# Shifted-window attention block on one core: moving a projection ahead of a weighed sum, norm sums ahead of an addition, and splitting an exp in two

## The chip, the cores and the metric

The kernel runs on one core of one Trainium2 chip. The metric is device time in microseconds (us), the median of several executions. Five engines take part, each with its own queue of instructions in program order: PE (TensorE: matmuls and transposes; its weight loads are shown apart as PEld), DVE (VectorE), ACT (ScalarE), POOL (GpSimd) and SP, which issues the DMAs. They are tied together by semaphores that the program sets by hand.

## The reference, cut to what matters

A block of a Swin-style transformer on x of shape (32, 32, 32, 64): 32 images of 32 x 32 tokens with 64 channels, windows of 8 x 8 tokens shifted by 4, 4 heads of 16.

```python
h = _ln(x, ln1_g, ln1_b); h = roll(h, (-4, -4)); win = windows(h, 8)     # 512 windows of 64 tokens
q, k, v = split(win @ qkv_w + qkv_b, 3)                                # per head 64 x 16
attn = softmax(q @ k.T * 16 ** -0.5 + rel_pos_bias + shift_mask)       # 64 x 64 per head
out = roll(unwindow((attn @ v) @ proj_w + proj_b), (4, 4))
x = x + out
h2 = _ln(x, ln2_g, ln2_b)
return x + gelu(h2 @ fc1_w + fc1_b) @ fc2_w + fc2_b
```

Everything is float32.

## The kernel before

The 32 images form 8 groups of 4. The attention half is one unrolled loop over `n`, 64 steps of half an image's windows ("pairs") and 4 more (`TAIL`) to drain; 8 steps make a group. Every engine has its own copy of the loop, and the order in which its code is written is the order of its queue. The feed-forward half (fc1, gelu, fc2) follows in a loop of its own.

On PE, one step holds some of these blocks:

- `score(image)`, at odd `n` alone: the 64 passes q·k for both pairs of the next image, into `scores[0]` and `scores[1]`. The keys come from `kX`, which SP's DMAs spread from `kT`.
- `weigh(n - 2)`: the weighed sum, probabilities times values, from `probsT` into `outs`. It waits for the exp of that pair (`probsT_ready`) and for the quotient before it (`outs_taken`).
- `fill(...)`: everything that uses the two PSUM banks `work`. `TASKS` lists them: "XT" (eight transposes of normed x), "QK" (queries and keys of one image), "V" (values), "Y" (output projection of half a group). A fill waits until the fill before it in the list was copied out of `work`: "QK" follows either an XT, which ACT copies (`xT_copied`), or a Y, which DVE adds to x (`y_added`); "V" follows a QK, which ACT copies (`kT`, then `qT`: `q_copied`).
- `transpose_probs(n - 1)`: eight 128 x 128 transposes of the shifted scores into `trans`, which are the same two banks as `scores[0]`. They wait for POOL's shift, for DVE's `scores_taken` on the image that was just scored, and for the exp of the pair before.
- `transpose_o(n - 3)`: two transposes of the quotient.

Per step, DVE runs `bias_and_max(n)` (L483 adds the bias to the scores, L489 takes row maxima), `divide(n - 3)` (L496, L498), at steps 7 and 1 of a group (counted from 0) `add_y` (L534, or three pieces at L540: adds the projection to x), `norm(n)` (sums for the layer norm: L412, L418), and at steps 3 and 5 `add_y_bias` (L524). POOL shifts the scores by the maxima (L373) and does the other steps of the norm. ACT runs the exp (L645: one instruction over `trans`, 1024 columns), copies the transposed quotient (L653) and empties `work` (L605 xT, L610 kT, L612 qT, L619 vX).

An XT stands at the end of steps 2 and 4 of a group, a Y at the end of steps 6 and 0, a QK in each odd step, a V after the transposes of each odd step. So in a steady group two of the four QKs follow an XT (steps 3 and 5) and two a Y (steps 7 and 1).

Of the kernel before, what the change touches and what calls it, by code (L numbers as in the profile page):

```python
# [8 lines left out]
ACT = mybir.ActivationFunctionType  # L9
# [3 lines left out]
P = 128  # L13
# [11 lines left out]
PAIRS = STEPS * GROUPS  # L25
BANK = 512
# [41 lines left out]
TR, PV, OUT = 1, 2, 3  # L68
# [33 lines left out]
def tasks_at(n):  # L102
    return [task[1:] for task in TASKS if task[0] == n]
# [12 lines left out]
def ln_at(stage, n):  # L116


    found = []
    for group in range(1, GROUPS + 1):  # L120
        steps = LN_STEPS_FIRST if group == 1 else LN_STEPS
        found += [(group, i) for i, at in enumerate(steps[stage])
                  if at is not None and STEPS * (group - 1) + at == n]
    return found
# [7 lines left out]
def build(nc, x_d, params_d, out_d):  # L132
    with ExitStack() as ctx:
        def sb(name, *shape, dtype=F32):
            return ctx.enter_context(nc.sbuf_tensor(name, [P, *shape], dtype))

        def sem(name):
            return ctx.enter_context(nc.semaphore(name))
# [6 lines left out]
        trans = scores[0]  # L145
# [12 lines left out]
        probs = [sb(f"probs{i}", 2 * BANK) for i in range(4)]  # L158
        probsT = [sb(f"probsT{i}", 2 * BANK) for i in range(2)]
# [13 lines left out]
        ident = sb("ident", P)  # L173
# [38 lines left out]
        trans_ready, probsT_ready = sem("trans_ready"), sem("probsT_ready")  # L212
# [39 lines left out]
        def means_before(G, i):  # L252

            if G == 0:
                return 1
            return 1 + 3 * (G - 1) + (1, 1, 2, 3)[i]
# [153 lines left out]
        def _(dve):  # L410
# [5 lines left out]
            def square_sum(u, r):  # L416
                dve.wait_ge(ln_squares, u + 1)
                nc.vector.tensor_reduce(stat_sq[:, r * WIN:(r + 1) * WIN],  # L418
                                        squares[r % PIECES][:, :].rearrange("q (a f) -> q a f", f=C),
                                        AXX, ALU.add).then_inc(ln_sq, 1)  # L420
# [7 lines left out]
            for t in range(2):  # L428
                done = nc.vector.memset(vX[t][:, :, :], 0.0)
# [4 lines left out]
            for column in ones:  # L434
                done = nc.vector.memset(column, 1.0)
# [6 lines left out]
            for half, i in ((second_half, 1), (first_half, 2), (second_half, 2), (first_half, 3),  # L442
                            (second_half, 3)):
                dst, src, c0, n = half(0, i)
                done = nc.vector.tensor_tensor(  # L445
                    dst, src.rearrange("q (a f) -> q a f", f=C),
                    stat_mean[:, c0:c0 + n].unsqueeze(2).to_broadcast([P, n, C]), ALU.add)
# [55 lines left out]
            def norm(n):  # L503
                for group, i in ln_at("square_sum", n):
                    square_sum(PIECES * group + i, i)
                for group, i in ln_at("sum", n):
                    if group == GROUPS:
                        sum2(i)
                        continue
                    if i == 0:  # L510
                        dve.wait_ge(x_loaded[group % 2], 16 * COPIES * (group // 2 + 1))
                        dve.wait_ge(ln_mean, means_before(group - 1, 3))
                    row_sum(x[:, group * ROW + i * PIECE:][:, 0:PIECE], i)

            def sum2(s):

                dve.wait_ge(ln_mean, MEANS + max(s - 3, 0))
                row_sum(x[:, s * PIECE:(s + 1) * PIECE], s % PIECES)
# [36 lines left out]
            for n in range(PAIRS + TAIL):  # L555
                if n < PAIRS:
                    bias_and_max(n)
                if 0 <= n - OUT < PAIRS:
                    divide(n - OUT)

                for kind, of, i in tasks_at(n - 0.5):
                    if kind == "Y":
                        add_y(of, i)
                norm(n)
                if n < PAIRS and n % STEPS in (3, 5):
                    add_y_bias(n // STEPS, (n % STEPS - 3) // 2)
            for kind, of, i in tasks_at(PAIRS + TAIL - 0.5):
# [24 lines left out]
        def _(act):  # L592
# [48 lines left out]
            squares_of(-1)  # L641

            def exp(n):
                act.wait_ge(trans_ready, n + 1)
                nc.scalar.activation(probsT[n % 2][:, :], trans, ACT.Exp)\  # L645
                  .then_inc(probsT_ready, 1)

            def copy_oT(n):
                act.wait_ge(oT_ready, n + 1)
# [45 lines left out]
        def _(pe):  # L695
            def mm(out, lhsT, rhs, start=True, stop=True):
                return nc.tensor.matmul(out, lhsT, rhs, start=start, stop=stop)  # L697
# [55 lines left out]
            for t in range(2):  # L753
                mm(scores2[:, 3 + t:4 + t], w1raw[0:C, t * P:(t + 1) * P], shift[0:C, 1:2], stop=False)
                done = mm(scores2[:, 3 + t:4 + t], ident[:, :], bf1_raw[:, t:t + 1], start=False)
# [9 lines left out]
            def score(image):  # L765

                two = image % 2
                if image:
                    pe.wait_ge(kX_loaded[two], 16 * KX_DMAS * ((image + 1) // 2))
                else:  # L770
                    pe.wait_ge(first_keys, 2)
                copied("QK", image // GI, image % GI)
                if image:
                    pe.wait_ge(scores_taken, 2 * image)
                if image > 1:
                    pe.wait_ge(probsT_ready, 2 * image - 2)
                for u in range(2):
                    for p in range(2):
                        for k in range(2):
                            at = (2 * k + u) * P + p * N  # L780
                            for w in range(2):
                                half = w ^ k
                                for hh in range(2):

                                    rows = slice(32 * (2 * w + hh), 32 * (2 * w + hh + 1))
                                    out = scores[k][half * N:(half + 1) * N, hh * BANK + u * 256:][:, 0:256]\
                                        .rearrange("q (h p m) -> q p h m", h=2, p=2)[:, p]
                                    done = mm(out, qT[two][rows, at:at + N], kX[two][rows, :, at:at + N])
                done.then_inc(scores_ready, 1)

            def transpose_probs(n, image):

                pe.wait_ge(shifted, n + 1)
                pe.wait_ge(scores_taken, 2 * image + 1)
                if n:
                    pe.wait_ge(probsT_ready, n)
                for t in range(8):
                    done = nc.tensor.transpose(trans[:, t * P:(t + 1) * P],  # L798
                                               probs[n % 4][:, t * P:(t + 1) * P], ident[:, :])
                done.then_inc(trans_ready, 1)  # L800

            def weigh(n):
                image, k = divmod(n, 2)
                if k == 0:
                    copied("V", image // GI, image % GI)
                pe.wait_ge(probsT_ready, n + 1)
                if n:
                    pe.wait_ge(outs_taken, n)
                else:
                    pe.wait_ge(y_bias_made, 1)  # L810
                for u in range(2):
                    for h in range(HEADS):
                        for w in range(2):
                            at = (u * HEADS + h) * P + (w ^ k) * N
                            row = (w * 4 + 2 * k + u) * HEADS + h
                            out = outs[w * N:(w + 1) * N, u * HEADS * VW:(u + 1) * HEADS * VW]\
                                .rearrange("q (p h d) -> q p h d", p=2, h=HEADS)[:, :, h]
                            done = mm(out, probsT[n % 2][:, at:at + N], vX[image % 2][:, row, :])
                done.then_inc(outs_ready, 1)
# [28 lines left out]
            for n in range(PAIRS + TAIL):  # L848
                if n % 2 and n + 1 < PAIRS:
                    score((n + 1) // 2)  # L850
                if 0 <= n - PV < PAIRS:
                    weigh(n - PV)
                if n % 2:
                    for kind, of, i in tasks_at(n):
                        fill(kind, of, i)
                if 0 <= n - TR < PAIRS:
                    transpose_probs(n - TR, min((n + 1) // 2, PAIRS // 2 - 1))
                if 0 <= n - OUT < PAIRS:
                    transpose_o(n - OUT)
                if n % 2 == 0:  # L860
                    for kind, of, i in tasks_at(n):
                        fill(kind, of, i)
                for kind, of, i in tasks_at(n + 0.5):
                    fill(kind, of, i)
                if n in (PAIRS, PAIRS + 1):
                    transpose_piece(n - PAIRS)

            pe.wait_ge(w1_ready, 1)
            pe.wait_ge(probsT_ready, PAIRS)
            pe.wait_ge(oT_copied, PAIRS)  # L870
            copied("Y", GROUPS - 1, 1)

# [74 lines left out]
```

## Time and profile before

| | us |
|---|---|
| median of 3 runs | 503.17 |
| the runs | 503.17, 503.45, 500.56 |
| the profiled execution | 500.17 |
| span in the profile | 498.4 |
| busy in the span: PE, DVE, POOL, ACT | 436.9, 383.7, 378.2, 294.9 |
| share of the chain that ended last: PE, DMA, ACT, DVE | 71%, 9%, 8%, 2% |

The profiled execution took 500.17 us, of which 1.8 us lie outside its span. The loop over pairs runs from about 34 us to 346 us of the span, the feed-forward half after it. "Idle before" in a row of a timeline is the time for which that engine had been idle, and the name behind the arrow is what ended it; "issue" stands there when the profile shows no releaser. The chain is the profile's walk back from the last instruction to what released each one.

### The profile page before, as it was taken

The numbers are of one execution on the slowest core, as the hardware profiler recorded it, in microseconds if no ns is written. First come the engines' busy times: TensorE is split into PE (matmuls) and PEld (weight loads), VectorE is DVE, ScalarE is ACT, GpSimd is POOL, SyncE is SP. The second block draws the span as 40 slices with busy tenths as digits, with TensorE's granted clock in tenths as the row PEclk, the third lists the DMA queues.
The fourth block names the chain that finished last, engine by engine and source line by source line (L and its number), as shares of the span: only waits on it lengthen the run. The fifth ranks groups of instructions, "written<-read, shape, count | busy, mean of one in ns | idle before, by whom it ended". The sixth has DMA issues, their size and how long they took to land.

```text
span 498.4 us, 21474 instructions
## 1 busy us (share of the span) xinstructions
PE 436.9 (88%) x9630; PEld 329.1 (66%) x9630; DVE 383.7 (77%) x549; ACT 294.9 (59%) x437; POOL 378.2 (76%) x376
## 2 busy tenths in 40 slices
PE   0665978899999899999999999787999999999995
PEld 0542756687777777777777767675566676667664
DVE  2767697889999999899999989965467766777652
ACT  1233665675765665666657646543777677767761
POOL 2658989988988989989889799730588888888830
PEclk9995999999999999999999999999999999999999
DMA  8300523511411511511111101100011321330333
GB/s 166 68 1 22 130 64 69 122 30 26 118 34 26 125 29 24 130 25 27 41 26 35 35 24 31 39 3 3 3 40 49 87 59 30 87 78 11 87 90 81
DMA packets 9986, 27.10 MB, mean 54 GB/s; under 512 B 3368, under 2 KB 3368, under 8 KB 7976
## 3 DMA queue, kind: packets, MB, share of 16 engines
q1 hardware_dynamic: 9896, 25.74, 22.0%
q8 instruction: 76, 1.25, 1.1%
q14 instruction: 14, 0.11, 0.1%
HBM read 9.21 MB, written 8.39 MB: 35 GB/s over the span
## 4 chain that ended last, share of the span: by engine, by line
PE 71%; DMA 9%; ACT 8%; SPq 4%; issue 4%; DVE 2%; ACTq 0%; DVEq 0%
PE work L697 26%; PE outs L697 17%; PE scores L697 16%; DMA kX<-kT 5%; PE scores L798 5%; ACT kT L610 4%; PE scores L838 4%; SPq L283 3%; DMA params<-in_params 2%; ACT qT L612 2%; PE work L712 2%; DMA x<-in_x 1%; PE outs L826 1%; ACT probsT L645 1%; SPq L275 1%
## 5 line engine op out<-in xcount | busy, mean ns | idle before, releaser
L373 POOL TENSOR_TENSOR probs<-probs,negmax 128x1024 f32<-128x1024 f32 x64 | 123.8, 1934 | 27.2 <-DVE negmax L489 27.1
L339 POOL TENSOR_TENSOR stat_rstd<-stat_var,minus_half 128x8 f32<-128x8 f32 (+1 forms) x62 | 104.9, 1691 | 5.0
L483 DVE TENSOR_TENSOR probs<-scores,bias 128x1024 f32<-128x1024 f32 x64 | 77.9, 1217 | 14.2 <-PE scores L697 14.2
L645 ACT ACTIVATE probsT<-scores 128x1024 f32<-128x1024 f32 x64 | 65.6, 1025 | 28.8 <-PE scores L798 28.8
L344 POOL TENSOR_TENSOR xn<-x,stat_mean 128x256 f32<-128x256 f32 (+1 forms) x91 | 78.1, 876 | 4.1
L697 PE MATMUL outs<-vX,probsT 128*64 128x34 f32 x2048 | 72.2, 225 | 9.4 <-issue 8.3
L489 DVE TENSOR_REDUCE negmax<-probs 128x16 f32<-128x1024 f32 x64 | 78.1, 1220 | 2.2
L697 PEld LDWEIGHTS outs<-vX,probsT 128*64 128x64 f32 x2048 | 65.9, 138 | 19.1 <-issue 19.0
L697 PEld LDWEIGHTS work<-params,probs 128*64 128x64 f32 x2048 | 62.3, 138 | 23.5 <-DVE x L577 20.5
L798 PEld LDWEIGHTS scores<-ident,probs 128*128 128x128 f32 x512 | 55.5, 142 | 28.1 <-issue 24.2
L610 ACT ACTIVATE kT<-work,bqkv 128x512 f32<-128x512 f32 x31 | 21.3, 688 | 86.6 <-PE work L697 86.6
L798 PE MATMUL scores<-ident,probs 128*128 128x128 f32 x512 | 70.6, 282 | 1.7 <-issue 1.7
L697 PE MATMUL work<-params,probs 128*64 128x64 f32 x2048 | 66.6, 223 | 0.0
L418 DVE TENSOR_REDUCE stat_sq<-squares 128x8 f32<-128x512 f32 x64 | 43.1, 681 | 28.2 <-ACT squares L597 28.0
L697 PE MATMUL scores<-kX,qT 32*64 32x128 f32 x2048 | 39.5, 282 | 15.6 <-DVE probs L483 5.6
L412 DVE TENSOR_REDUCE stat_sum<-x 128x8 f32<-128x512 f32 x64 | 42.2, 676 | 9.6 <-DMA x<-in_x 9.5
L597 ACT ACTIVATE squares<-xn 128x512 f32<-128x512 f32 x64 | 39.7, 630 | 15.7 <-DVE xn L445 15.3
L682 ACT ACTIVATE probs<-scores,bf 128x1024 f32<-128x1024 f32 x32 | 35.6, 1114 | 20.9 <-PE scores L697 20.8
L336 POOL TENSOR_TENSOR stat_var<-stat_sq,eps 128x8 f32<-128x8 f32 (+1 forms) x62 | 23.2, 375 | 31.6 <-DVE stat_sq L418 31.6
L697 PEld LDWEIGHTS scores<-kX,qT 32*64 32x64 f32 x2048 | 32.0, 133 | 22.5 <-DMA kX<-kT 14.5
L329 POOL TENSOR_TENSOR stat_mean<-stat_sum,one_over_c 128x8 f32<-128x8 f32 (+2 forms) x54 | 17.4, 322 | 33.6 <-DVE stat_sum L412 30.4
L619 ACT ACTIVATE vX<-work 64x512 f32<-64x512 f32 x64 | 39.0, 610 | 4.8 <-PE work L697 4.4
(61 smaller groups left out, 662.4 us busy)
## 6 DMA issues: line engine op xcount, KB each, us to landing
kX<-kT SPq DMA_DIRECT2D x124, 64.0 KB, 2.0
x<-in_x SPq DMA_DIRECT2D x32, 224.0 KB
out<-x SPq DMA_DIRECT2D x28, 224.0 KB
x<-in_x SPq DMA_DIRECT2D x32, 32.0 KB
out<-x SPq DMA_DIRECT2D x28, 32.0 KB
out<-x SPq DMA_DIRECT2D x16, 56.0 KB
params<-in_params SPq DMA_DIRECT2D x1, 805.5 KB, 12.0
out<-x SPq DMA_DIRECT2D x16, 8.0 KB
```

What stands on the lines that cost most here:

```text
L339: nc.gpsimd.tensor_tensor(stat_rstd[:, cols], stat_var[:, cols], minus_half[:, cols], ALU.pow).then_inc(ln_rstd, pieces)
L344: return nc.gpsimd.tensor_tensor(dst, src.rearrange("q (a f) -> q a f", f=C), m, ALU.add)
L373: nc.gpsimd.tensor_tensor(e, e, top, ALU.add).then_inc(shifted, 1)
L412: nc.vector.tensor_reduce(stat_sum[:, r * WIN:(r + 1) * WIN], src.rearrange("q (a f) -> q a f", f=C), AXX, ALU.add, negate=True).then_inc( ...
L418: nc.vector.tensor_reduce(stat_sq[:, r * WIN:(r + 1) * WIN], squares[r % PIECES][:, :].rearrange("q (a f) -> q a f", f=C), AXX, ALU.add).t ...
L483: nc.vector.tensor_tensor(e[:, :].rearrange("q (u a m) -> q a u m", u=2, a=2), scores[k].rearrange("q (a u m) -> q a u m", a=2, u=2), b.re ...
L489: nc.vector.tensor_reduce(negmax[n % 4][:, :], e[:, :].rearrange("q (a m) -> q a m", m=N), AXX, ALU.max, negate=True).then_inc(negmax_read ...
L597: nc.scalar.activation(squares[j % PIECES][:, :], xn[:, j * PIECE:(j + 1) * PIECE], ACT.Square, scale=float(C) ** -0.5).then_inc(ln_square ...
L610: nc.scalar.activation(kT[par][:, :], work[1], ACT.Identity, bias=bqkv[:, 1:2])\
L645: nc.scalar.activation(probsT[n % 2][:, :], trans, ACT.Exp)\
L697: return nc.tensor.matmul(out, lhsT, rhs, start=start, stop=stop)
L798: done = nc.tensor.transpose(trans[:, t * P:(t + 1) * P], probs[n % 4][:, t * P:(t + 1) * P], ident[:, :])
```

## The change

PE: in an odd step the fills of whole number `n` (the QK) now stand ahead of `weigh` and no longer behind it. ACT: the exp is two instructions of 512 columns, and each waits for its own four transposes. PE's transposes signal after every four, and each four wait for the half of the exp before that read their bank; `weigh` waits for one half ahead of each half of its matmuls. DVE: `norm(n)` now stands ahead of `add_y`. The work done is otherwise the same.

```diff
@@ DVE
+                norm(n)
                 for kind, of, i in tasks_at(n - 0.5):
                     if kind == "Y":
                         add_y(of, i)
-                norm(n)
@@ ACT
             def exp(n):
-                act.wait_ge(trans_ready, n + 1)
-                nc.scalar.activation(probsT[n % 2][:, :], trans, ACT.Exp)\
-                  .then_inc(probsT_ready, 1)
+                for half in range(2):
+                    cols = slice(half * BANK, (half + 1) * BANK)
+                    act.wait_ge(trans_ready, 2 * n + half + 1)
+                    nc.scalar.activation(probsT[n % 2][:, cols], trans[:, cols], ACT.Exp)\
+                      .then_inc(probsT_ready, 1)
@@ PE, score and transpose_probs
-                    pe.wait_ge(probsT_ready, 2 * image - 2)
+                    pe.wait_ge(probsT_ready, 2 * (2 * image - 2))
...
-                if n:
-                    pe.wait_ge(probsT_ready, n)
-                for t in range(8):
-                    done = nc.tensor.transpose(trans[:, t * P:(t + 1) * P],
-                                               probs[n % 4][:, t * P:(t + 1) * P], ident[:, :])
-                done.then_inc(trans_ready, 1)
+                for half in range(2):
+                    if n:
+                        pe.wait_ge(probsT_ready, 2 * n - 1 + half)
+                    for t in range(4 * half, 4 * (half + 1)):
+                        done = nc.tensor.transpose(trans[:, t * P:(t + 1) * P],
+                                                   probs[n % 4][:, t * P:(t + 1) * P], ident[:, :])
+                    done.then_inc(trans_ready, 1)
@@ PE, weigh
-                pe.wait_ge(probsT_ready, n + 1)
...
                 for u in range(2):
+                    pe.wait_ge(probsT_ready, 2 * n + u + 1)
@@ PE, the loop
-                if 0 <= n - PV < PAIRS:
-                    weigh(n - PV)
                 if n % 2:
                     for kind, of, i in tasks_at(n):
                         fill(kind, of, i)
+                if 0 <= n - PV < PAIRS:
+                    weigh(n - PV)
```

On PE, in step 7 of a group, behind a Y (`work<-params,oT`): the queue before, with what each block waits for. `work<-xT,wqkv` is the QK, `outs<-vX,probsT` the weighed sum, L798 the transposes.

```order
167 L697 MATMUL work<-params,oT 64x64 x31
168 L697 MATMUL scores<-kX,qT 64x2x64 [waits scores_taken,probsT_ready,q_copied,kX_loaded0]
169 L697 MATMUL scores<-kX,qT 64x2x64 x31
170 L697 MATMUL outs<-vX,probsT 64x2x17 [waits outs_taken,probsT_ready]
171 L697 MATMUL outs<-vX,probsT 64x2x17 x15
172 L697 MATMUL work<-xT,wqkv 64x512 [waits y_added]
173 L697 MATMUL work<-xT,wqkv 64x512 x3
174 L798 MATMUL scores<-ident,probs 128x128 [waits probsT_ready,scores_taken,shifted]
175 L798 MATMUL scores<-ident,probs 128x128 x7
```

And the same place now (line numbers are shifted by two or three):

```order
219 L699 MATMUL work<-params,oT 64x64 x31
220 L699 MATMUL scores<-kX,qT 64x2x64 [waits scores_taken,probsT_ready,q_copied,kX_loaded0]
221 L699 MATMUL scores<-kX,qT 64x2x64 x31
222 L699 MATMUL work<-xT,wqkv 64x512 [waits y_added]
223 L699 MATMUL work<-xT,wqkv 64x512 x3
224 L699 MATMUL outs<-vX,probsT 64x2x17 [waits probsT_ready,outs_taken]
225 L699 MATMUL outs<-vX,probsT 64x2x17 x7
226 L699 MATMUL outs<-vX,probsT 64x2x17 [waits probsT_ready]
227 L699 MATMUL outs<-vX,probsT 64x2x17 x7
228 L801 MATMUL scores<-ident,probs 128x128 [waits probsT_ready,scores_taken,shifted]
229 L801 MATMUL scores<-ident,probs 128x128 x3
230 L801 MATMUL scores<-ident,probs 128x128 [waits probsT_ready]
```

The QK with its wait for `y_added` has moved up by one block, so that only the scores stand between the Y and it, and the weighed sum is queued behind it.

On DVE, the same step before, from the quotient to the next scores:

```order
220 L498 TENSOR_TENSOR o_rows<-outs,inverse 128x256
221 L534 TENSOR_TENSOR x<-work,x 128x2x512
222 L418 TENSOR_REDUCE stat_sq<-squares 128x8
223 L483 TENSOR_TENSOR probs<-scores,bias 128x2x2x256
224 L489 TENSOR_REDUCE negmax<-probs 128x16
```

Now:

```order
220 L498 TENSOR_TENSOR o_rows<-outs,inverse 128x256
221 L418 TENSOR_REDUCE stat_sq<-squares 128x8
222 L534 TENSOR_TENSOR x<-work,x 128x2x512
223 L483 TENSOR_TENSOR probs<-scores,bias 128x2x2x256
224 L489 TENSOR_REDUCE negmax<-probs 128x16
```

The norm's sum and the addition to x have changed places.

## Rows read from the trace of the kernel before

**Rows 1.** Busy us of each engine in one stretch: start:end, length, then PE, PEld, DVE, ACT, POOL.

```profile
222.00:254.00 32.00, 30.24 (x763) 23.97 (x758) 29.82 (x40) 19.17 (x32) 28.07 (x26) 1.00 0.11 28
```

**Rows 2.** Timeline of PE, one image with an XT ahead: start, us, line, what.

```profile
204.00 1.21 PE L697 MATMUL scores<-kX,qT 32*64 32x128 f32 x64 [0.56 <-DMA kX<-kT]
205.13 1.13 PE L697 MATMUL outs<-vX,probsT 128*64 128x34 f32 x32
...
207.21 1.09 PE L798 MATMUL scores<-ident,probs 128*128 128x128 f32 x8
208.14 0.38 PE L826 MATMUL outs<-ident,o_rows 128*128 128x128 f32 x2
208.66 0.70 PE L697 MATMUL work<-wqkv,xT 64*64 64x64 f32 x32
209.63 1.13 PE L697 MATMUL outs<-vX,probsT 128*64 128x34 f32 x32 [0.27 <-issue]
...
211.61 0.38 PE L826 MATMUL outs<-ident,o_rows 128*128 128x128 f32 x2
211.83 1.04 PE L712 MATMUL work<-ident,xn 128*128 128x128 f32 x8
212.99 1.20 PE L697 MATMUL scores<-kX,qT 32*64 32x128 f32 x64
```

**Rows 3.** Timeline of ACT in the same stretch.

```profile
207.93 0.68 ACT L612 ACTIVATE qT<-work,bqkv 128x512 f32<-128x512 f32 x1
208.50 1.02 ACT L645 ACTIVATE probsT<-scores 128x1024 f32<-128x1024 f32 x1
209.41 0.39 ACT L653 ACTIVATE oT<-outs 128x256 f32<-128x256 f32 x1
...
211.81 1.03 ACT L645 ACTIVATE probsT<-scores 128x1024 f32<-128x1024 f32 x1 [0.91 <-PE scores L798]
...
213.00 1.03 ACT L605 ACTIVATE xT<-work 128x1024 f32<-128x1024 f32 x1
```

**Rows 4.** Waits of the whole span: total us, times, longest.

```profile
PE outs L697 <- issue: 8.3, 28, 0.9
...
PE scores L697 <- DMA kX<-kT: 3.8, 7, 1.3
PE scores L697 <- ACT probsT L645: 3.3, 4, 1.0
```

**Rows 5.** Timeline of DVE, steps 5 to 1 of that group.

```profile
213.05 1.93 DVE L524 TENSOR_TENSOR x<-x,y_bias 128x1024 f32<-128x1024 f32 x1
214.90 1.21 DVE L483 TENSOR_TENSOR probs<-scores,bias 128x1024 f32<-128x1024 f32 x1
...
222.13 1.23 DVE L534 TENSOR_TENSOR x<-work,x 128x1024 f32<-128x1024 f32 x1 [0.54 <-PE work L697]
223.27 0.68 DVE L418 TENSOR_REDUCE stat_sq<-squares 128x8 f32<-128x512 f32 x1
223.87 1.21 DVE L483 TENSOR_TENSOR probs<-scores,bias 128x1024 f32<-128x1024 f32 x1
...
231.15 1.36 DVE L540 TENSOR_TENSOR x<-work,x 128x512 f32<-128x512 f32 x3 [0.59 <-PE work L697]
```

**Rows 6.** Timeline of PE, later blocks of that group and the next group's scores.

```profile
216.22 1.06 PE L798 MATMUL scores<-ident,probs 128*128 128x128 f32 x8
...
222.00 1.21 PE L697 MATMUL scores<-kX,qT 32*64 32x128 f32 x64
...
240.60 1.21 PE L697 MATMUL scores<-kX,qT 32*64 32x128 f32 x64 [0.36 <-DMA kX<-kT]
```

**Rows 7.** Timeline of POOL around the row of 213.05 us above.

```profile
212.00 1.90 POOL L373 TENSOR_TENSOR probs<-probs,negmax 128x1024 f32<-128x1024 f32 x1 [0.28 <-DVE negmax L489]
213.86 1.18 POOL L329 TENSOR_TENSOR stat_mean<-stat_sum,one_over_c 128x8 f32<-128x8 f32 x1
```

**Rows 8.** Timeline of DVE early in the loop.

```profile
60.63 1.28 DVE L412 TENSOR_REDUCE stat_sum<-x 128x8 f32<-128x512 f32 x2 [1.89 <-DMA x<-in_x]
```

More of the change, by code:

```diff
@@ L868, in _ @@
             pe.wait_ge(w1_ready, 1)
-            pe.wait_ge(probsT_ready, PAIRS)
+            pe.wait_ge(probsT_ready, 2 * PAIRS)
             pe.wait_ge(oT_copied, PAIRS)
```

## The prediction

> **What bounds the kernel now.** I read the shares of the chain first: 71% of what ended last is PE. Then the busy time of each engine in a stretch of the loop [rows 1]: of 32 us PE is busy 30.24, DVE 29.82, POOL 28.07, ACT 19.17. So two engines are nearly full: PE can give back at most 1.8 us in 32, DVE 2.2. A change of order can therefore bring some per cent of the loop and no more, and what PE wins DVE must be able to follow. The feed-forward half behind the loop is not touched.
>
> Next the timeline of PE over one image of two steps [rows 2], from one start of scores (204.00) to the next (212.99): 8.99 us. Two places are not back to back. The transposes of the quotient take .22 us from start to next start where nothing waits (211.61 to 211.83), but .52 in the odd step (208.14 to 208.66): the V behind them lost .30 us. ACT shows why [rows 3]: its copy of the queries ran from 207.93 for .68, to 208.61, and V started .05 later. The second place is the weighed sum of the even step at 209.63, idle before it .27. ACT's exp ran from 208.50 for 1.02, to 209.52; the sum started .11 later. Both come from the late QK: the exp stands behind the two copies on ACT, and it could start at 208.50 because the copy before it was issued out only then. The list of waits [rows 4] shows the second place 28 times in the span, 8.3 us in total. Two waits of the scores are beside it: for the keys' DMA 3.8 us in 7 times, for the exp 3.3 in 4.
>
> **The change part by part.**
>
> QK ahead of the weighed sum. Nothing is added; QK and weighed sum take 2.08 us together (205.13 to 207.21 [rows 2]) in either order. The QK starts about 1.05 us earlier, so the copies of keys and queries end that much earlier, and V no longer waits: .30 won. The exp then starts as soon as its transposes are done. Its DMAs go with it: SP spreads the keys 1.05 us earlier, and the scores' waits for them (.56 and .36 in [rows 2, 6]) are covered but for the longest of 1.3: of 3.8 us I take 3.4 as won.
>
> The exp in halves. Shown is the price of a 1024-column exp, .91 us from start to next start (208.50 to 209.41), and of a 512-column instruction, .57 (207.93 to 208.50) with .68 of duration [rows 3]. Two halves thus cost 1.14, .23 more, 64 times 15 us of ACT; ACT is idle 12.8 of 32 us [rows 1], and the copies behind the exp in the even step wait for PE anyway (xT at 213.00, as XT ends [rows 2, 3]). If that cover were gone, it would be .23 per step. The first half is due .46 earlier (four transposes of .116), so with the odd exp freed the weighed sum finds its first half done: PE comes to it .93 + .22 + .70 = 1.85 us after the transposes' start, the half is ready after about 1.4, the second at 2.0 against 2.4 wanted. That wins the .27. Behind an even step without a fill the scores wait for the whole exp: its end comes .23 earlier (start .11 later than now, .68 instead of 1.02), 4 times: .9.
>
> So the gaps: 28 x (.27 + .30) = 16.0 us; with 3.4 and .9, 20.3 us. Extra waits on PE cost between nothing and the .05 by which V lagged its releaser; I take nothing, since each is long met when PE comes to it.
>
> What is late next. First, the QK now has only the scores between itself and the fill before it. Behind an XT: XT starts at 211.83, its copy runs 213.00 to 214.03 [rows 3]; the QK comes at 212.99 + 1.13 = 214.12. Just met, nothing lost. Behind a Y: the QK waits for DVE's addition, and the weighed sum, the transposes and V are queued behind it. Second, the odd transposes wait until DVE has read the new scores, and DVE does not get faster.
>
> I follow one group from the scores at step 3 (204.00 is 0). DVE's chain from there: L483 of step 6 at 10.90 [rows 5], ending 12.11, without a pause before it, so the transposes of step 5 stay at 12.22 [rows 6] although PE comes there .57 earlier: this image's first .57 is lost. From there 5.78 us to the scores of step 7 (216.22 to 222.00) become 5.21: 17.43. DVE is free for its addition at 222.13 - .54, that is 17.59, as before. The norm's sum goes first (.60 from start to start, [rows 5]): 18.19, then the addition, 1.23: done 19.42, QK at 19.5. PE was there at 17.43 + 1.13 = 18.56: it waits .95. Transposes at 19.5 + 2.08 = 21.6, scores of step 1 at 26.8. There L540 takes 1.36: DVE is free at 26.6, the addition ends 28.2, QK at 28.3, PE there at 27.9: it waits .37. Transposes 30.4, and the next group's first scores 5.21 later at 35.6, before 36.60 [rows 6]: 1.0 us a group. The norm's sum ahead brings L483 of the next step .60 earlier on DVE, where it is not awaited, and costs PE up to .60 at step 7: alone it brings nothing.
>
> Summed over the loop: six groups have both Ys, 6 x (.95 + .37) = 7.9 us lost; six groups lose .57 in the transposes of step 5, 3.4 us; and what the first two images win is lost where DVE waits for x from HBM until 60.63 [rows 8], 1.1 us. 20.3 - 12.4 = 7.9 us won, 8 in round figures. On the profiled execution, 500.17, that gives 492.2; on the median of the runs, 503.17, 495.2. Since the three runs lie in two places (500.6, and 503.2 to 503.5), I forecast between the two, **493.7 us**. Its own range: three to twelve won, 488.5 to 498.5.
>
> **A rule against the trace.** The .57 of step 5 and most of the .95 hang on L524, which took 1.93 us at 213.05 beside POOL's L373 (212.00 to 213.90 [rows 5, 7]); POOL's next small operation took 1.18 and ended .06 after L524. It looks as if one waited for the other to end. The Trainium skill, SBUF — State Buffer, "SBUF: two separate sides", says just this: the port pair that VectorE and GpSimd share is held for a whole instruction, by an operation of two SBUF inputs too, and the other blocks. By that rule the stretch stays, since L373 starts when the maxima of the same step are done and L524 1.1 us later in either order, and the sum stays 8; by a sharing of bandwidth it would depend on the load and could go, which is the third rival.
>
> **The rivals.**
>
> The fill takes it all. If DVE comes to its additions .7 us later than the rows say, each of 12 QKs waits .7 more: 12 x .7 = 8.4, and nothing is left: 499.5 to 503. For it: DVE is at 93% [rows 1]. Against: it had been idle .54 and .59 before its additions [rows 5]. Chance .11.
>
> The halves open nothing. The even weighed sum waits for the quotient as well as for the exp; if the quotient ends last, 28 x .27 = 7.6 us of the sum are gone: 499.8 to 502.8. Against: the sum starts .11 after the exp's end in the image shown, as it must if the exp releases it. Chance .05.
>
> DVE has more room. If L524 falls beside no POOL operation that reads much, it takes 1.2 instead of 1.93, and .7 in each of six groups come off DVE's chain: 3.4 of step 5 and some 3 of the waits at step 7 come back, 14 us won: 486 to 488.5. For it: POOL is near its own bound and its phase may shift. Chance .11.
>
> Slower: the QK behind a Y holds up PE. Before, weighed sum and scores, 2.2 us, stood between Y and QK; now 1.13. If the wait grew by 1.3 us at 12 places over my .66 on average, 15.6 us, it would outweigh the 7.9 and cost 8 more; it turns to a loss from .66 more on, and to one of 1% (5 us, about what a measurement of this kernel can tell from no change) from 1.1 more. DVE would have to be late by that much at an addition for which it now waits: 505 to 510. Chance .04.
>
> **How the numbers follow.** Forecast .69, the rivals .11, .05, .11, .04. The range takes in the forecast's own and part of the cases on both sides: 487 to 499.5. Faster by over 1% (under 498.1): nearly all of .69 and the .11 of the third rival, .79. Within 1%: the first two rivals and the forecast's edge, .17. Slower by over 1%: .04.
>
> **What the profile will show.** Right: the even weighed sum has no idle time before it; V follows the quotient's transposes after .22; image to image 8.4 us behind an XT where DVE is not late; QKs behind a Y wait .4 to 1 us for DVE, with the transposes of step 5 waiting for L483; DVE's idle time in the stretch of rows 1 falls under 1.5 us; the exp shows 128 instructions of about .65. Wrong: if the scores go on waiting for the keys, if DVE newly waits for the weighed sum (which ends 1.05 later in the odd step and leaves some .05 us behind a Y), or if PE's gaps stay where they were.

## The result, and the profile after

| | before | changed |
|---|---|---|
| median, us | 501.87 | 488.44 |
| runs | 500.45 to 503.45 | 486.25 to 491.11 |
| profiled execution (span) | 500.17 (498.4) | 491.11 (489.2) |

The ratio is 0.9744, with a 95% interval from 0.9697 to 0.979: 13.4 us faster by the medians. A few executions, mostly of the kernel before, ran some per cent slower throughout; the ratios here and below leave them out, the medians do not. Forecast were 493.7 in a range of 487 to 499.5, so the time lies inside, nearer the low end, and the gain was sized too small: 8 against 13.

The chain that ended last by engine, from the page of the profile after:

```profile
PE 64%; DVE 22%; DMA 5%; issue 3%; ACT 2%; SPq 2%; ACTq 0%; DVEq 0%
```

DVE's share was 2%; now a fifth of what ends last is DVE. The stretch that answers to [rows 1]:

```profile
222.00:254.00 32.00, 30.65 (x842) 25.15 (x838) 30.63 (x42) 22.82 (x43) 29.81 (x31) 1.00 0.14 34
```

DVE's idle time in 32 us fell from 2.2 to 1.4. The PE timeline of one group, which answers to [rows 2] and [rows 6]:

```profile
198.96 1.21 PE L699 MATMUL scores<-kX,qT 32*64 32x128 f32 x64 [0.24 <-DMA kX<-kT]
...
203.10 0.38 PE L829 MATMUL outs<-ident,o_rows 128*128 128x128 f32 x2
203.41 0.69 PE L699 MATMUL work<-wqkv,xT 64*64 64x64 f32 x32
204.04 1.13 PE L699 MATMUL outs<-vX,probsT 128*64 128x34 f32 x32
...
206.02 0.38 PE L829 MATMUL outs<-ident,o_rows 128*128 128x128 f32 x2
206.24 1.04 PE L714 MATMUL work<-ident,xn 128*128 128x128 f32 x8
207.21 1.21 PE L699 MATMUL scores<-kX,qT 32*64 32x128 f32 x64
208.48 1.09 PE L699 MATMUL work<-xT,wqkv 64*64 64x512 f32 x8
...
211.17 1.06 PE L801 MATMUL scores<-ident,probs 128*128 128x128 f32 x8 [0.54 <-issue]
...
216.44 1.21 PE L699 MATMUL scores<-kX,qT 32*64 32x128 f32 x64
218.33 1.09 PE L699 MATMUL work<-xT,wqkv 64*64 64x512 f32 x8 [0.68 <-DVE x L534]
...
225.76 1.38 PE L699 MATMUL scores<-kX,qT 32*64 32x128 f32 x64
227.21 1.09 PE L699 MATMUL work<-xT,wqkv 64*64 64x512 f32 x8
...
234.32 1.21 PE L699 MATMUL scores<-kX,qT 32*64 32x128 f32 x64
```

Both gaps have gone: V follows the quotient's transposes after .31, the weighed sum has no idle time before it. The three new waits of the forecast stand there: the transposes of step 5 (.54), the QK of step 7 (.68, for `x L534`), and at step 1 the QK a little later than its scores end (225.76 + 1.38 to 227.21). DVE in the same group, to be held against [rows 5]:

```profile
208.01 1.93 DVE L524 TENSOR_TENSOR x<-x,y_bias 128x1024 f32<-128x1024 f32 x1
209.86 1.21 DVE L483 TENSOR_TENSOR probs<-scores,bias 128x1024 f32<-128x1024 f32 x1
...
216.47 0.68 DVE L418 TENSOR_REDUCE stat_sq<-squares 128x8 f32<-128x512 f32 x1
217.06 1.22 DVE L534 TENSOR_TENSOR x<-work,x 128x1024 f32<-128x1024 f32 x1
```

In this group DVE no longer waits ahead of L534 (over the span its waits there went from 8.3 us in 8 times to 3.2 in 3); the norm's sum stands between it and the quotient, and PE waits for what follows.

The group against the forecast, each time counted from its first scores (198.96):

| event | forecast | measured |
|---|---|---|
| scores of step 5 | 8.42 | 8.25 |
| transposes of step 5 | 12.22 | 12.21 |
| scores of step 7 | 17.43 | 17.48 |
| QK of step 7 | 19.5 | 19.37 |
| scores of step 1 | 26.8 | 26.80 |
| QK of step 1 | 28.3 | 28.25 |
| next group's scores | 35.6 | 35.36 |

On ACT the exp is 128 instructions of .60 us, where about .65 was forecast:

```profile
L647 ACT ACTIVATE probsT<-scores 128x512 f32<-128x512 f32 x128 | 69.7, 595 | 29.1 <-PE scores L801 28.7
```

The profiled execution is the slowest of the four. Two stretches of it ran at TensorE's lower level (1.2 GHz). Before kept 1.00 at the first place; at its first feed-forward matmuls, which answer to the second, it had .63. Stretches of the kernel before and of the changed one, columns as in [rows 1] with the granted clock third from the end:

```profile
346.00:350.00 4.00, 2.44 (x6) 1.28 (x8) 3.18 (x6) 0.33 (x1) 1.79 (x3) 0.63 0.00 0
```

```profile
72.00:76.00 4.00, 3.65 (x49) 3.21 (x54) 2.44 (x5) 2.65 (x6) 3.92 (x6) 0.50 0.64 143
...
336.00:342.00 6.00, 5.16 (x14) 2.38 (x16) 2.47 (x5) 2.45 (x3) 2.83 (x4) 0.50 0.00 0
```

### The profile page after: what moved, and what is told of

It is laid out like the page before. It is cut to its first block, busy times and chain, and to the rows that moved or that the text cites. A ratio compares the mean times of both kernels' runs of the same rounds, so it can differ in the third digit from the quotient of the medians.

```text
span 489.2 us, 21538 instructions
## 1 busy us (share of the span) xinstructions
PE 437.2 (89%) x9630; PEld 331.7 (68%) x9630; DVE 383.4 (78%) x549; ACT 306.1 (63%) x501; POOL 378.1 (77%) x376
## 4 chain that ended last, share of the span: by engine, by line
PE 64%; DVE 22%; DMA 5%; issue 3%; ACT 2%; SPq 2%; ACTq 0%; DVEq 0%
PE work L699 23%; PE outs L699 14%; PE scores L699 13%; PE scores L801 7%; DVE probs L483 5%; DVE negmax L489 5%; PE scores L841 4%; DVE stat_sum L412 3%; DMA params<-in_params 2%; DVE x L524 2%; DVE x L540 2%; DVE x L534 2%; PE outs L829 2%; PE work L714 1%; DMA kX<-kT 1%
## 5 line engine op out<-in xcount | busy, mean ns | idle before, releaser
L373 POOL TENSOR_TENSOR probs<-probs,negmax 128x1024 f32<-128x1024 f32 x64 | 123.0, 1924 | 21.6 <-DVE negmax L489 21.6
L647 ACT ACTIVATE probsT<-scores 128x512 f32<-128x512 f32 x128 | 69.7, 595 | 29.1 <-PE scores L801 28.7
L483 DVE TENSOR_TENSOR probs<-scores,bias 128x1024 f32<-128x1024 f32 x64 | 77.9, 1217 | 11.7 <-PE scores L699 11.6
L801 PE MATMUL scores<-ident,probs 128*128 128x128 f32 x512 | 71.5, 284 | 4.6 <-issue 4.6
L801 PEld LDWEIGHTS scores<-ident,probs 128*128 128x128 f32 x512 | 56.2, 143 | 9.2 <-issue 5.1
L684 ACT ACTIVATE probs<-scores,bf 128x1024 f32<-128x1024 f32 x32 | 35.6, 1114 | 22.8 <-PE scores L699 22.8
L336 POOL TENSOR_TENSOR stat_var<-stat_sq,eps 128x8 f32<-128x8 f32 (+1 forms) x62 | 24.3, 391 | 27.9 <-DVE stat_sq L418 27.9
L699 PE MATMUL work<-xT,wqkv 64*64 64x512 f32 x256 | 36.6, 628 | 7.6 <-DVE x L534 3.0
```

The costliest lines, as they stand in the source:

```text
L373: nc.gpsimd.tensor_tensor(e, e, top, ALU.add).then_inc(shifted, 1)
L483: nc.vector.tensor_tensor(e[:, :].rearrange("q (u a m) -> q a u m", u=2, a=2), scores[k].rearrange("q (a u m) -> q a u m", a=2, u=2), b.re ...
L647: nc.scalar.activation(probsT[n % 2][:, cols], trans[:, cols], ACT.Exp)\
L684: nc.scalar.activation(hidden[s % 2][half][:, :], fc1_bank[half][:, :], ACT.Gelu_apprx_tanh, bias=bf1[:, half:half + 1])\
L801: done = nc.tensor.transpose(trans[:, t * P:(t + 1) * P], probs[n % 4][:, t * P:(t + 1) * P], ident[:, :])
```

## The experiments

Each was timed in five rounds against the kernel before, on the chip of its group. The first four ran together, the next four together, then the last three.

**The changed kernel again (c_after).** No edit.

> The changed kernel again, unaltered, as the measure for the other runs. Theory A (the schedule of the prediction is right, and the profiled execution of the changed kernel lost some 4 us to a lower granted clock at 68 to 77 and 331 to 344 us): an execution with the clock up there takes 485.5 to 487.5, and image to image in the loop stays 35.4 to 35.7 us a group. Theory B (the clock is the same in all executions and the spread is something else): the profile repeats the half clock at both places, and the times stay about 488 to 491.

Measured: ratio 0.9771 (0.9731 to 0.9812), median 488.6; the profiled execution took 487.65 at a mean clock of .988 (before: 500.17 at .985). From 199.18 to 234.54, a group is 35.36 us. At 330 to 342 us the granted clock is now 1.00, at 60 to 70 us it is .83. So the clock differs between executions, as theory A has it, though it was not up everywhere, and the time is .15 above theory A's range. This execution, 12.5 us under that of before at nearly the same mean clock, is the one for a budget. Its waits on PE, in total us, times, longest:

```profile
PE scores L699 <- DVE probs L483: 7.9, 2, 5.6
PE work L699 <- DVE x L534: 4.9, 7, 1.3
...
PE scores L801 <- issue: 3.2, 6, 0.7
PE scores L699 <- ACT probsT L647: 2.4, 3, 0.9
...
PE work L699 <- DVE x L540: 1.6, 5, 0.3
PE scores L699 <- DMA kX<-kT: 1.4, 3, 0.8
```

**Queries and keys ahead alone (q_only).**

```diff
-                if 0 <= n - PV < PAIRS:
-                    weigh(n - PV)
                 if n % 2:
                     for kind, of, i in tasks_at(n):
                         fill(kind, of, i)
+                if 0 <= n - PV < PAIRS:
+                    weigh(n - PV)
```

> Queries and keys ahead of the weighed sum alone; exp whole, norm sums behind the addition. Theory A (the gaps belong together): V no longer waits for the copies, but the whole exp now ends last, so the even weighed sum waits about .40 us instead of .27; a group goes from 36.6 to about 36.1 us, the kernel to 496.5 to 499. Theory B (the move alone is the change, the halves only add instructions): 489 to 492.

Measured: ratio 0.9916 (0.9879 to 0.9952), median 497.59, 4.2 us. PE's timeline of an image with an XT ahead:

```profile
208.29 0.38 PE L826 MATMUL outs<-ident,o_rows 128*128 128x128 f32 x2
208.60 0.69 PE L697 MATMUL work<-wqkv,xT 64*64 64x64 f32 x32
209.61 0.60 PE L697 MATMUL outs<-vX,probsT 128*64 128x34 f32 x14 [0.32 <-issue]
...
211.81 1.04 PE L712 MATMUL work<-ident,xn 128*128 128x128 f32 x8
212.97 1.20 PE L697 MATMUL scores<-kX,qT 32*64 32x128 f32 x64
```

V comes .31 after the quotient's transposes, but the weighed sum still waits, .32 (some .40 expected): theory A. The keys' DMA is gone from the waits of PE, so the early QK does carry its DMAs.

**The exp in halves alone (halves_only).** The changed kernel with the QK and the norm sums put back.

> The exp in halves alone; queries and keys stay behind the weighed sum, norm sums behind the addition. Theory A: the even weighed sum loses its wait (.27 us at 28 places), V keeps its .30, and the scores of steps 1 and 3 go on waiting for the keys' DMA, which starts where it did; some .5 us a group, the kernel 495.5 to 498.5. Theory B (the halves are the change): 489 to 492.

Measured: ratio 0.9847 (0.9803 to 0.989), median 493.47, 7.7 us by the ratio. That is between the theories, and more than theory A allows. Its timeline shows why:

```profile
205.16 0.38 PE L829 MATMUL outs<-ident,o_rows 128*128 128x128 f32 x2
205.69 0.69 PE L699 MATMUL work<-wqkv,xT 64*64 64x64 f32 x32
206.31 1.13 PE L699 MATMUL outs<-vX,probsT 128*64 128x34 f32 x32
...
208.52 1.04 PE L714 MATMUL work<-ident,xn 128*128 128x128 f32 x8
209.48 0.83 PE L699 MATMUL scores<-kX,qT 32*64 32x128 f32 x37
```

V keeps its .53 behind the quotient's transposes, as expected. But V to weighed sum is .62, where it was .97 [rows 2], a gain of .35 and not .27; and XT to scores is .96, where it was 1.16 [rows 2] and is 1.16 above with the whole exp. Those .20 us were a wait of the scores for the exp, in each image behind an XT, that no list shows: before, the exp ended at 212.84 [rows 3] and the scores came at 212.99, and XT's bar is drawn 1.04 long, so that only .12 of the 1.16 shows as a gap. How much earlier the exp ends is seen behind an even step's transposes, in before:

```profile
210.68 1.09 PE L798 MATMUL scores<-ident,probs 128*128 128x128 f32 x8
```

and here (the second row is both halves):

```profile
207.37 1.09 PE L801 MATMUL scores<-ident,probs 128*128 128x128 f32 x8
208.06 1.09 ACT L647 ACTIVATE probsT<-scores 128x512 f32<-128x512 f32 x2
```

The whole exp began 1.13 us after the transposes (211.81 [rows 3]) and ended 2.16 after them; the halves begin .69 after and end 1.78 after. PE still waits for the keys' DMA, now 8.8 us in 13 times where it was 3.8 in 7, so that part of what the halves win is lost there.

**Norm sums ahead alone (norm_only).**

```diff
+                norm(n)
                 for kind, of, i in tasks_at(n - 0.5):
                     if kind == "Y":
                         add_y(of, i)
-                norm(n)
```

> Norm sums ahead of the addition to x alone. Theory A (the sum fills DVE's wait for the projection, but nobody waits for what it brings forward): 500.5 to 503.5, no change. Theory B (DVE bounds the loop, and .6 us at 12 places come back): 495 to 498.

Measured: ratio 1.0002 (0.9966 to 1.0039), median 501.34: nothing. Theory A. The three parts alone make 7.7 + 4.2 + 0 = 11.9 of the whole change's 11.5 to 13.4.

**The changed kernel without the norm part (no_norm).** The diff above, undone.

> The changed kernel with the norm sums back behind the addition to x. Theory A (prediction: the sum ahead costs PE up to .6 us at step 7, since the QK behind the Y waits for the addition and DVE is then late): the QK of step 7 waits some .1 to .3 us instead of .61 to .68, a group takes 34.7 to 34.9 us instead of 35.4, and the kernel 484.5 to 486 against 488.6 of the changed kernel. Theory B (the sum ahead is part of the gain, since DVE is the bound): 489 to 492.

Measured: ratio 0.9717 (0.9681 to 0.9753), median 486.3, against 0.9771 and 488.6 of the changed kernel. The time is .3 above the expected range, and the intervals overlap; what tells the theories apart is the place itself, step 7 in PE's timeline:

```profile
214.41 1.09 PE L699 MATMUL work<-xT,wqkv 64*64 64x512 f32 x8 [0.16 <-DVE x L534]
```

The QK waits .16 where it waited .68, and the group from 195.52 to 230.41 takes 34.89 us in place of 35.36. So beside the other two parts the norm sums ahead cost some 2 us (nn_early against early, below, has 2.8). Theory B is out. The other two parts together win 14.2 us by the ratio, where apart they make 11.9; that fits the keys, for which halves_only waits 8.8 us and this run 2.2, and was not tried by itself.

**add_y_bias at steps 2 and 3 (bias23).** Against the changed kernel:

```diff
-                if n < PAIRS and n % STEPS in (3, 5):
-                    add_y_bias(n // STEPS, (n % STEPS - 3) // 2)
+                if n < PAIRS and n % STEPS in (2, 3):
+                    add_y_bias(n // STEPS, n % STEPS - 2)
```

> The changed kernel with the second half of add_y_bias moved from step 5 to step 2 (half 0 at step 2, half 1 at step 3). Theory A (L524 took 1.93 us because POOL's L373 had begun and it waited for that to end): at step 2 L373 begins after the maxima too, so L524 is stretched there to 2.2 to 2.5 us, DVE is late by over 1 us at the scores of step 3, and the kernel gains nothing: 487 to 491. Theory B (the stretch belongs to step 5's load, or is none of POOL's): L524 takes 1.2 at both places, the transposes of step 5 no longer wait, a group takes 34.2 us, the kernel 480.5 to 483.

Measured: ratio 1.0049 (1.0013 to 1.0084), median 504.16: all of the change's gain and more is gone. The mechanism is theory A's, its price was far too low. POOL and DVE at one place:

```profile
198.87 1.90 POOL L373 TENSOR_TENSOR probs<-probs,negmax 128x1024 f32<-128x1024 f32 x1
...
204.61 1.90 POOL L373 TENSOR_TENSOR probs<-probs,negmax 128x1024 f32<-128x1024 f32 x1
```

```profile
199.28 2.57 DVE L524 TENSOR_TENSOR x<-x,y_bias 128x1024 f32<-128x1024 f32 x1
...
204.78 2.81 DVE L524 TENSOR_TENSOR x<-x,y_bias 128x1024 f32<-128x1024 f32 x1
```

Both times L524 ends 1.08 us after L373 does (200.77 and 201.85; 206.51 and 207.59); alone it takes 1.22, so nearly all its work came after L373's end. The move stretched the untouched half too (step 3, 1.22 us in the changed kernel), since it shifted step 3 to where L373 had just begun. PE's transposes of step 3 then waited 2.28 us:

```profile
208.83 1.94 PE L801 MATMUL scores<-ident,probs 128*128 128x128 f32 x8 [2.28 <-issue]
```

Here the granted clock was .50 from 208.8 to 210.8 us, and the eight transposes took 1.94 us. Over the span PE waited ahead of the transposes of the scores

```profile
PE scores L801 <- issue: 16.6, 9, 2.3
```

where c_after had 3.2 us in 6 times: most of what was lost.

**x of group 2 loaded early (early).** Against the changed kernel:

```diff
             load(1)
+            load(2)
             sp.wait_ge(zeroed, 2)
...
-                if n in (1, STEPS - 2):
-                    load(2 if n == 1 else 3)
+                if n == STEPS - 2:
+                    load(3)
```

> The changed kernel with the load of x for group 2 issued behind that of group 1 instead of in step 1. Theory A (what the first images win is lost where DVE waits 4 us for x, and the clock is lost there too): no wait for x at 60 us, the interval of the scores there falls from 11.2 to 8.3 to 9.2 us, the kernel 484 to 486.5. Theory B (something else ends last there, keys or x of another group): 488 to 490.

Measured: ratio 0.9676 (0.9634 to 0.9717), median 483.95, some 4.6 us under the changed kernel. DVE comes to the sum of [rows 8] with no wait:

```profile
57.32 1.27 DVE L413 TENSOR_REDUCE stat_sum<-x 128x8 f32<-128x512 f32 x2
```

The interval of the scores there falls from 11.25 in c_after (53.10 to 64.35) to 8.48 (53.07 to 61.55), and the next from 10.42 (to 74.77) to 8.49 (to 70.04): 4.7 us, all of the gain. Theory A.

**Both (nn_early).** The last two edits together.

> Both together: norm sums back behind the addition, and the early load. Theory A: both gains add, since they lie in different groups: 480.5 to 483. Theory B of either: 486 to 490.

Measured: ratio 0.9624 (0.9589 to 0.9659), median 481.17. Theory A: the two add. Against early, timed beside it, the norm sums behind the addition win 2.8 us.

**One wait ahead of the whole weighed sum (late_gate).** Against the changed kernel, in `weigh`:

```diff
+                pe.wait_ge(probsT_ready, 2 * n + 2)
                 if n:
                     pe.wait_ge(outs_taken, n)
...
                 for u in range(2):
-                    pe.wait_ge(probsT_ready, 2 * n + u + 1)
```

> The changed kernel, with the weighed sum waiting for both halves of the exp ahead of its first matmul. Theory A (what the halves win is that the exp starts behind four transposes; in the trace of the changed kernel both halves end 1.79 us after the transposes' start, and PE comes to the weighed sum at 1.87): nearly nothing is lost, 488 to 490. Theory B (the split wait in the weighed sum wins the .27 to .35 us): 496 to 499.

Measured: ratio 0.9764 (0.9731 to 0.9797), median 489.86: within a microsecond or so of the changed kernel. PE's timeline in an even step:

```profile
201.69 0.69 PE L699 MATMUL work<-wqkv,xT 64*64 64x64 f32 x32
202.32 1.13 PE L699 MATMUL outs<-vX,probsT 128*64 128x34 f32 x32
```

V to weighed sum is .63, as in the changed kernel (203.41 to 204.04). Theory A: the halves win by starting behind four transposes; that the weighed sum waits for them one by one wins nothing that shows.

**add_y_bias ahead of the quotient (swap).** Against the changed kernel, on DVE:

```diff
                     bias_and_max(n)
+                if n < PAIRS and n % STEPS in (3, 5):
+                    add_y_bias(n // STEPS, (n % STEPS - 3) // 2)
                 if 0 <= n - OUT < PAIRS:
                     divide(n - OUT)
...
-                if n < PAIRS and n % STEPS in (3, 5):
-                    add_y_bias(n // STEPS, (n % STEPS - 3) // 2)
```

> The changed kernel with add_y_bias between the row maxima and the quotient on DVE. Theory A (L524 waits only for a L373 that began before it; issued right behind the maxima it comes first, takes 1.2 us, and L373 waits instead, which has slack): the transposes of step 5 no longer wait .5 us, a group takes some .7 us less, the kernel 483 to 485.5. Theory B (L373 still comes first, or POOL's delay is what is late next): L524 takes 2.2 to 2.8 us, 489 to 500.

Measured: ratio 0.9654 (0.9628 to 0.968), median 483.06. Theory A. DVE at step 5, then POOL:

```profile
202.57 1.22 DVE L524 TENSOR_TENSOR x<-x,y_bias 128x1024 f32<-128x1024 f32 x1
```

```profile
202.73 2.81 POOL L373 TENSOR_TENSOR probs<-probs,negmax 128x1024 f32<-128x1024 f32 x1
```

Now L524 begins .16 before L373, runs its 1.22, and L373 is the one that is stretched, to 2.81. POOL has the room: between 94 and 300 us PE's waits no longer list the transposes of the scores (`scores L801`) at all, and the group from 194.74 to 229.39 takes 34.65 us in place of 35.36.

**The three together (best).** nn_early with the edit of swap.

> Norm sums behind the addition, early load of x, and add_y_bias ahead of the quotient together. Theory A (the three gains lie at different places of the chain): 475.5 to 478.5. Theory B (one of them only moves the wait): 480 to 484.

Measured: ratio 0.9553 (0.9528 to 0.9578), median 478.63, just above theory A's range and below theory B's: 22 us under the kernel before, 10 under the changed one.

## Why the prediction was right, and where its sizes were off

**Where the number fell.** The whole range holds it, but the forecast's own, three to twelve won and 488.5 to 498.5, does not quite: 13.4 were won by the medians. It is inside because the range was opened towards the third rival (486 to 488.5), and that is luck: the number is that rival's, its condition did not come true (L524 took 1.93 us at step 5 of the group shown, as before). The mechanism was forecast, its size was not.

**The two gaps and their cause** were right. V waited for the copies and the weighed sum for the exp; both waits went, and q_only and halves_only take them away one at a time (.31 for V with the QK moved, .62 from V to the sum with the exp halved).

**The size of the gaps** was right in sum, .56 for .57 an image, though not one by one: taken were .30 and .27, measured .21 (.52 to .31) and .35 (.97 to .62). V cannot follow after .22, which was the step to an XT: to a V it is .31 in every image of c_after. The .9 for four scores without a fill ahead was measured too. What the sum lacked is .20 more in the 14 images behind an XT, where the scores waited for the exp unseen. I had read "XT to scores" as back to back because the row showed no idle time; the start-to-start time of 1.16 against eight transposes of .116 had .2 us to spare. The prediction let the weighed sum start on a finished first half, with the second ending 2.0 us after the transposes' start; the second ended some 1.8 after, PE came 1.87 after (202.17 to 204.04 in the changed kernel), and late_gate shows that nothing hung on the first alone. Nor did the halves cost ACT .23 us a pair: from start to next start the pair takes .97 (208.06 to 209.03 in halves_only), .06 more than the whole exp.

**What is late next** was right in each place and dear by some: for the two QKs behind a Y .95 and .37 were taken. Start to start, less the 1.13 of the scores, the group above gives .76 (216.44 to 218.33) and .32 (225.76 to 227.21): the first came .13 us earlier after its group's first scores than reckoned. The lists give less, .68 and little or nothing, since idle time counts only from the end of the scores' bar. XT's copy, which I had called just met, now costs .14 (207.21 to 208.48, 1.27 against 1.13), because the scores ahead of it come .2 earlier.

**The keys** were sized too high: 3.4 of 3.8 us were taken as won, 1.4 is left, so 2.4.

**The first images** were rightly seen as held by x's load, at 1.1 us; the new wait of PE for DVE's L483 there is 7.9 - 5.6 = 2.3 us.

The budget of c_after against the profile of before, with these values: gaps 28 x .56 = 15.7, scores behind XT 14 x .20 = 2.8, keys 2.4, scores behind the whole exp 3.3 - 2.4 = .9; less the transposes' waits 3.2 - 1.7 (which before had mostly in one place) = 1.5, the QKs behind Y 4.9 + 1.6 - 1.3 (one at the loop's end stood before as well) = 5.2, and the first images 2.3. That is 21.8 - 9.0 = 12.8 us; the two profiled executions are 12.5 apart. The sum is good to some 1.5 us only: the losses are listed waits, and counted from start to start they are 1 to 2 us more. The stretch from the first scores to the first matmul of the feed-forward half (44.06 to 347.56 before, 44.53 to 336.26 in c_after) is 11.8 shorter; c_after's first scores came .5 later, and its first feed-forward matmuls were 1.4 us shorter (336.26 to 338.18, before 347.56 to 350.89) where before's granted clock was .63 (346 to 350 us). So the loop itself gave some 12, and the sum holds within its error. The prediction had 20.3 - 12.4: it won 1.5 too little, and lost too much by 1.4 to 3.4.

**The norm sums ahead** were judged rightly: alone nothing (norm_only), and a cost of up to .60 at step 7; the group in no_norm is .47 shorter without them.

**The lock behind L524** was the rule weighed against the trace, and it holds: bias23 and swap move who comes first, and the other is stretched. The third rival's condition, a stretch that would go by itself, did not come true; but its price, 3.4 and some 3 us, nearly did, once swap took the stretch away on purpose (5.5 us).

**The forecast between the two places of before's runs** turned out to be part of a wider spread, of which the granted clock in two stretches is a part shown by the profiles of the changed kernel; the rest of the spread was not followed up.

## What to carry to other kernels

Read gaps from start to start against the same pair of blocks elsewhere in the loop: a wait of .2 us can hide under a bar and be in every second image. When a producer is cut in halves so that it can start early, the early start is the gain; a split wait at the consumer may add nothing. And when the bounding engine has been freed, follow one period by hand through the next engine's queue: here that gave each event to .3 us, and it pointed to two of the three edits that together won 10 us more (the third came from a wait for x early in the loop). It also pointed to bias23, which lost 16: before an operation is moved, see what runs beside it at its new place.

## What the runs showed of the hardware

Of VectorE's addition L524, which has two SBUF inputs, and GpSimd's L373 the one that began second did nearly all its work after the other's end. L524 took 1.22 us where it began first or alone and, begun behind L373, 1.93, 2.57 or 2.81, each time ending 1.08 after L373's end; L373 took 1.90 and, behind L524 in swap, 2.81, ending 1.75 after L524. The Trainium skill, SBUF — State Buffer, "SBUF: two separate sides", says that the two hold a shared port pair for a whole instruction and do not share it, and the runs agree. Not expected was how little decides: in swap L524 is .16 us ahead, and that order at step 5 is worth some 5 us of the kernel.

TensorE's granted clock fell to its lower level (1.2 GHz) in some executions behind waits of PE, and stayed up in others behind the same waits. In the changed kernel's PE timeline:

```profile
63.24 1.20 PE L699 MATMUL scores<-kX,qT 32*64 32x128 f32 x64 [1.75 <-DVE probs L483]
...
68.53 1.06 PE L801 MATMUL scores<-ident,probs 128*128 128x128 f32 x8 [2.02 <-issue]
```

From 72 to 76 us the clock was then .50. In c_after, at the same place, the scores at 64.35 took 1.79 behind a wait of 2.24, and the QK after them 1.99, where 1.09 is usual (clock .83 from 60 to 70). But no_norm has nearly the same two waits and kept 1.00 from 60 to 80 us:

```profile
63.38 1.20 PE L699 MATMUL scores<-kX,qT 32*64 32x128 f32 x64 [1.84 <-DVE probs L483]
...
68.68 1.06 PE L801 MATMUL scores<-ident,probs 128*128 128x128 f32 x8 [2.02 <-issue]
```

In bias23 the transposes took 1.94 us behind the waits at 96.28 and 208.83 (2.31 and 2.28), and 1.07 and 1.06 behind the same wait at 134.57 and 171.87 (2.31 each). And at the end of the loop after and c_after have the same three waits (.56, 1.34, 1.68) ahead of a clock of .50 and of 1.00. So the wait alone does not tell what the clock does next; what does stays open. Nor is the clock the main price of the wait for x: over the two images behind it c_after takes 21.67 us (53.10 to 74.77), no_norm with the clock up 20.98 (52.82 to 73.80), early without the wait 16.97 (53.07 to 70.04).
